# Moving the s dot products to GpSimd and ScalarE, the weight parts into the attention loop, and the denominators to tiny matmuls, in a graph-attention kernel

## The chip, the cores and the metric

The kernel runs on one core of one Trainium2 chip. The metric is the device time of one execution in microseconds (us), lower is better. TensorE is the matmul engine (PE in the rows, PEld its weight loads), VectorE is DVE, ScalarE is ACT, GpSimd is POOL, and SyncE (SP) issues the transfers. Each engine runs its own queue in order, and semaphores order them against each other.

## The reference

There are N = 1250 nodes with D = 512 features and 20,000 edges. A layer norm and a relu give h. The first layer is graph attention followed by a spline layer, the second is three graph convolutions with batch norm. The change lies in the first:

```python
HW = h @ W
s = HW @ a[:OUT_F, 0]
t = HW @ a[OUT_F:, 0]
e = leaky_relu(s[row] + t[col], negative_slope=0.2)
m = segment_max(e, row); ex = exp(e - m[row])
den = segment_sum(ex, row); att = ex / den[row]
agg = segment_sum(att[:, None] * h[col], row)
basis = _b_splines(agg, grid)
out = silu(agg) @ base_w.T + einsum('nip,oip->no', basis, spline_w)
```

## The kernel before, in words

Nodes are held as NT = 10 tiles of 128. The 20,000 edges become a dense count matrix C16 (f16), built by VectorE's one-hots and TensorE in 20 groups and copied out of PSUM by ScalarE (0 to 69 us). ScalarE's statistics, the normalised rows `hx` and their f16 high part `hH` are made beside it.

Then the attention scores. s and t are dot products of each row of hx with a row vector; TensorE made the two vectors in PSUM banks 6 and 7 and ScalarE copied them to WAB. VectorE's `projections(k, t0, t1)` makes one sum per node tile (L925). TensorE's `spread` turns a column of per-node values into a row on all partitions (L1328). VectorE takes the largest |t|, ScalarE adds twice that to the row of t (U), and per tile VectorE's `mask` (L950) and `largest` (L958) find the largest t over each node's edges. `columns` (L964 to L969) turns the maxima of a set of tiles (SETS, of 4, 3 and 3 tiles) into two columns P and Q, TensorE spreads them, ScalarE copies them out (`attention_rows`). Meanwhile TensorE transposes C16 and ScalarE copies the result to CT (`transposed`), TensorE sums the degrees with 100 matmuls of one column (`degrees`), and ScalarE sums the squares of the spline weights WKf, nine pieces of 1024 KB (`sum_squares`), from which one scale for the weights follows.

The attention loop runs n over 3 groups of destinations (G = 418 columns each) times 10 source tiles. Each iteration is `attention_sum(n+1)` (VectorE, L987), `exponentials` (ScalarE, L590), `attention_f32` (VectorE, L999: times the counts), a cast to f16 (ScalarE, L599, high part into CT) and `attention_low` (VectorE, L994, low part). In the first ten iterations VectorE also makes `hL`, the low part of the features (`feature_rest`, L1004). TensorE follows with `attend(g, k, j)`: k = 1 to 4 are the feature chunks of 128, three matmuls each, and k = 0 are the denominators, two matmuls with a matrix of ones, all of 418 columns; a group is 10 x 14 matmuls. The last three tiles of a group (LASTS) run chunk by chunk, so that chunks end one after another. VectorE then takes the reciprocal of the denominators (`denominators`, L1027 and L1029) and scales the chunks (`aggregated`, L1035).

After the loop ScalarE and VectorE split the spline weights into high and low f16 parts (`weights_high` L606, `weights_low` L1040; units 0 to 9, the others at LATE_TURN inside the turns), interleaved with `silu_of`, `silu_high` and `silu_low`. Each spline unit is 24 matmuls of 418 columns (L1482). TensorE runs four silu units first (`silu_units`), then 8 turns of two units for each group. A turn's operands go through ScalarE's `middle`, `nearest`, `clipped`, `squares_of`, `turn_high` (L620, L625, L631 and L632, L644 and L647, L665) and VectorE's `cube_outer`, `cube_inner`, `spline`, `turn_low`, `upper`, `lower` (L1048, L1051, L1055, L1072, L1083, L1089). The tiles kr, ka and kb of a turn share memory with hH and hL, so `middle(0)` waits until TensorE has finished the aggregation. Layer norm and the three graph convolutions follow.

## Time and profile before

| what | value |
|---|---|
| median of 3 runs | 684.4 us (683.07 to 684.95) |
| the profiled execution's own time | 683.7 us |
| its span, first to last instruction | 681.9 us |
| mean granted TensorE clock | 0.95 of full speed |
| busy, share of the span | TensorE 604.3 us (89%), VectorE 477.9 (70%), ScalarE 371.5 (54%), GpSimd 23.3 (3%) |
| chain that ended last, by engine | TensorE 67%, VectorE 18%, ScalarE 8%, issue 4% |

Busy time is an average over stages with different bounds. The chain is followed back from the last instruction, at each step to what released it. A matmul's end is modelled, so successive starts tell more than the duration of one. The granted clock has two levels, 2.4 GHz (1.00) and 1.2 GHz (0.50).

### The profile page before, as it was taken

Reading aid. Unit: us, or ns where it says so; the run is one execution under the profiler, and the core shown is the slowest. Engines: PE = TensorE matmul, PEld = TensorE weight load, DVE = VectorE, ACT = ScalarE, POOL = GpSimd, SP = SyncE. Lnnn points to the kernel's source line nnn. Section 1 sums busy time; section 2 is a strip of 40 time slices with the busy share of each in tenths; the row PEclk is TensorE's granted clock in tenths of the full one; section 3 lists DMA queues with packets and bytes.
Section 4 is the critical chain, followed back from the end, with each engine's and each line's share of the span. In section 5 each row is a group of like instructions: output and inputs, shape, how many; then the busy total and the mean of one; then the engine's idle time right before and its main releaser. Section 6 shows DMA issues by size and latency. Waiting matters only on the chain.

```text
span 681.9 us, 8727 instructions
## 1 busy us (share of the span) xinstructions
PE 604.3 (89%) x3437; PEld 428.2 (63%) x3437; DVE 477.9 (70%) x739; ACT 371.5 (54%) x486; POOL 23.3 (3%) x30
## 2 busy tenths in 40 slices
PE   3766655999968999999999999869999999999994
PEld 2535643555534455555555555448999899988994
DVE  7989698999785999997369865784344434542354
ACT  1798597545779998987198620328331422332111
POOL 2000000000000000000000000202300020000000
PEclk9798686999979899999999999979999999999998
DMA  8553400000040000000001000090100000001202
GB/s 278 192 186 126 195 1 0 1 1 1 0 151 0 2 1 0 1 1 1 1 1 62 1 0 1 23 369 15 62 1 1 0 1 1 1 0 56 94 38 113
DMA packets 11417, 33.73 MB, mean 49 GB/s; under 512 B 718, under 2 KB 1038, under 8 KB 11120
## 3 DMA queue, kind: packets, MB, share of 16 engines
q1 hardware_dynamic: 11376, 33.17, 13.8%
q8 instruction: 27, 0.44, 0.3%
q14 instruction: 14, 0.11, 0.1%
HBM read 24.78 MB, written 8.40 MB: 49 GB/s over the span
## 4 chain that ended last, share of the span: by engine, by line
PE 67%; DVE 18%; ACT 8%; issue 4%; DVEq 1%; ACTq 1%; DMA 0%; SPq 0%
PE bank L1482 32%; PE bank L1557 20%; PE bank L1526 12%; DVE AL L994 2%; DVE OR L847 2%; DVE OM L850 2%; DVE EX L987 1%; DVE EX L999 1%; DVE SCR L958 1%; ACT CT L599 1%; PE bank L1328 1%; ACT JSQ L532 1%; ACT WKh L606 1%; DVE RDN L1029 1%; DVE hL L1004 1%
## 5 line engine op out<-in xcount | busy, mean ns | idle before, releaser
L1482 PE MATMUL bank<-BHL,WKh 128*128 128x418 f16 x1152 | 207.1, 342 | 4.2 <-DVE BHL L1083 4.2
L1482 PEld LDWEIGHTS bank<-BHL,WKh 128*128 128x128 f16 x1152 | 112.0, 97 | 99.3 <-DVE BHL L1083 4.6
L1557 PE MATMUL bank<-CF,YL 128*128 128x418 f32 x360 | 127.5, 354 | 0.0
L1557 PE MATMUL bank<-CF,YH 128*128 128x418 f32 x360 | 126.6, 352 | 0.0
L1277 DVE TENSOR_TENSOR Z<-bank,dvb 128x418 f32<-128x418 f32 x36 | 21.3, 593 | 69.1 <-PE bank L1557 69.1
L1557 PEld LDWEIGHTS bank<-CF,YL 128*128 128x128 f32 x360 | 67.6, 188 | 1.8
L1557 PEld LDWEIGHTS bank<-CF,YH 128*128 128x128 f32 x360 | 67.7, 188 | 1.0
L784 ACT ACTIVATE bnc<-bnm,tiny 128x1 f32<-128x1 f32 x12 | 3.5, 294 | 104.9 <-DVE bnm L1283 104.9
L1335 PE MATMUL bank<-OM,OR 128*128 128x160 f16 x320 | 32.3, 268 | 19.7 <-DVE OM L850 13.7
L1228 DVE SCALAR_TENSOR_TENSOR YL<-bank,dvc,YH 128x512 fp32r<-128x512 f32 x30 | 21.9, 748 | 38.5 <-ACT YH L765 38.5
L1526 PE MATMUL bank<-GWH,XH 128*128 128x512 f32 x120 | 48.1, 401 | 0.0
L1526 PE MATMUL bank<-GWL,XH 128*128 128x512 f32 x120 | 46.9, 391 | 0.0
L1526 PE MATMUL bank<-GWH,XL 128*128 128x512 f32 x120 | 46.9, 391 | 0.0
L1335 PEld LDWEIGHTS bank<-OM,OR 128*128 128x128 f16 x320 | 27.9, 114 | 29.0 <-DVE OM L850 26.2
L1427 PE MATMUL bank<-CT,hH 128*128 128x418 f16 x120 | 41.3, 344 | 0.0
L1427 PE MATMUL bank<-CT,hL 128*128 128x418 f16 x120 | 41.2, 344 | 0.0
L1427 PE MATMUL bank<-AL,hH 128*128 128x418 f16 x120 | 41.2, 344 | 0.0
L765 ACT ACTIVATE YH<-bank,dvc 128x512 fp32r<-128x512 f32 x30 | 20.7, 692 | 33.2 <-PE bank L1526 33.2
L1089 DVE TENSOR_TENSOR BHL<-kh,BHL 128x1672 f16<-128x1672 f16 x24 | 24.7, 1029 | 19.6 <-PE bank L1482 19.6
L1482 PE MATMUL bank<-BHL,WK 128*128 128x418 f16 x144 | 28.4, 361 | 6.4 <-issue 6.4
L644 ACT ACTIVATE ks<-kx 128x836 f32<-128x836 f32 x24 | 21.5, 897 | 17.4 <-DVE kh L1072 15.9
L850 DVE TENSOR_TENSOR OM<-iota,kwin 128x2560 f16<-128x2560 f16 x20 | 29.6, 1478 | 0.0
(202 smaller groups left out, 1010.6 us busy)
## 6 DMA issues: line engine op xcount, KB each, us to landing
WKf<-in_wk SPq DMA_DIRECT2D x9, 1024.0 KB, 5.4
c_scratch<-C SPq DMA_DIRECT2D x1, 3200.0 KB, 10.9
GWf<-in_gwT SPq DMA_DIRECT2D x3, 1024.0 KB, 5.4
C<-c_scratch SPq DMA_DIRECT2D x1, 2880.0 KB, 10.4
XT<-in_xT SPq DMA_DIRECT2D x1, 2500.0 KB, 8.8
x_scratch<-XT SPq DMA_DIRECT2D x1, 2500.0 KB, 16.1
XR<-x_scratch SPq DMA_DIRECT2D x1, 2500.0 KB, 8.9
outT<-Z SPq DMA_DIRECT2D x4, 625.0 KB, 3.1
```

The costliest lines, as they stand in the source:

```text
L644: nc.scalar.activation(ks(i)[:, :], ka[:, n % 2, :], ACT.Square, scale=(1.0 / 6.0) ** 0.5)
L765: nc.scalar.mul(YH[:, t, :], bank[:, t % YB, :], dvc[:, t:t + 1]).then_inc(y_high, 1)
L847: V.tensor_tensor(fours(OR[:, buf, :, :]), rows_of(iota[:, 0:P], VIS), fanned(index, P), ALU.is_equal)
L850: V.tensor_tensor(fours(OM[:, buf, :, :]), rows_of(iota[:, :], VIS), fanned(index, MOV), ALU.is_equal).then_inc(ready, 1)
L1089: V.tensor_tensor(both(u + 1), kh[n % 2], both(u), ALU.subtract).then_inc(k_lower, 1)
L1228: V.scalar_tensor_tensor(YL[:, t, :], bank[:, t % YB, :], dvc[:, t:t + 1], YH[:, t, :].bitcast(F32), ALU.mult, ALU.subtract).then_inc(y_lo ...
L1277: V.tensor_tensor(Z[:, c, g * G:(g + 1) * G], bank[:, YB + u % YB, 0:G], dvb[:, g * G:(g + 1) * G], ALU.mult).then_inc(z_out, 1)
L1335: ins = mm(out, OR[:, buf, v0 + v, :], OM[:, buf, v0 + v, :], start=(first and v == 0), stop=(last and v == n - 1))
L1427: ins = mm(bank[:, ((DC + 1) * g + k) % 8, 0:G], lhs, m[:, j, cols], start=(j == 0 and i == 0), stop=(j == NT - 1 and i == len(parts) - 1))
L1482: ins = mm(bank[:, 4 * (g % 2) + o, 0:G], lhs, rhs, start=(u == 0 and q == 0 and i == 0), stop=(u == UNITS - 1 and q == PAIR - 1 and i == 2))
L1526: ins = mm(bank[:, t % YB, :], lhs, rhs[:, c, :], start=(c == 0 and i == 0), stop=(c == DC - 1 and i == 2))
L1557: ins = mm(bank[:, YB + u % YB, 0:G], Y[:, j, o * P:(o + 1) * P], CF[:, j, g * G:(g + 1) * G], start=(j == 0 and i == 0), stop=(j == NT - ...
```

## The change

- The ten products for s are made by GpSimd (`product`) in three buffers SH, and summed by ScalarE while it copies them in place (`projected`). GpSimd also makes hL (`feature_rest`). VectorE keeps the t sums, which read their vector from PSUM.
- The largest |t| is replaced by a bound: ScalarE takes the norm of the vector for t during the counting. The bound is added to t's column before it is spread, and the masks read the spread row from PSUM; U is gone. TensorE transposes through banks 4 and 5 alone, and spreads t, then sums degrees, behind tile 0.
- Six sums of squares move from ahead of the loop into iterations 0, 2, 4, 6, 8 and 10; the table for Exp is loaded before the first rows of P and Q.
- The denominators are made with the weights as the stationary operand and one column of ones: 80 matmuls of one column for a group (`weight_sums`), a reciprocal of 4 columns, and a spread (`sums_spread`).
- Ten high parts and eight low parts of the spline weights move into the loop; behind it stand the silu steps alone, and the order of the first turns' steps on ScalarE is changed.

```diff
+LATE_SQUARES = (0, 2, 4, 6, 8, 10)
...
+DEN_AT = 480
+BOUND = 1.02
+FIRST_HALF = 16
...
-LATE_TURN = (0, 1, 2, 3, 4, 5, 5, 6)
+LOOP_LOWS = 8
+LATE_TURN = (1, 2, 2, 3, 3, 4, 5, 6)
...
+        SH = at("SH", Z4 + 9600, [LOT, D], F32)
+        WA = at("WA", Z4 + 12552, [D], F32)
+        SCR = at("SCR", Z4 + 8320, [2, NP], F16)
...
+            def feature_rest(t):
+                pool.wait_ge(h_high, t + 1)
+                nc.gpsimd.tensor_tensor(hL[:, t, :], hx[:, t, :], hH[:, t, :], ALU.subtract).then_inc(h_low, 1)
+
+            def product(t):
+                pool.wait_ge(h_rows, t + 1)
+                if t >= LOT:
+                    pool.wait_ge(s_sums, t - LOT + 1)
+                nc.gpsimd.tensor_tensor(SH[:, t % LOT, :], hx[:, t, :], WA[:, :], ALU.mult).then_inc(s_products, 1)
+
+            pool.wait_ge(sub_counted, GROUPS)
+            pool.wait_ge(wa_set, 1)
+            for t in range(NT):
+                product(t)
+            pool.wait_ge(t_cols, 1)
+            for t in range(NT):
+                feature_rest(t)
...
-                    nc.scalar.copy(WAB[:, :, :], bank[:, 6:8, :]).then_inc(wa_set, 1)
+                    nc.scalar.copy(WA[:, :], bank[:, 6, :]).then_inc(wa_set, 1)
+                    nc.scalar.activation(JST[:, 0, :], bank[:, 7, :], ACT.Square, accum_out=tb[:, 0:1])
+                    act.drain()
+                    nc.scalar.activation(tb[:, 1:2], tb[:, 0:1], ACT.Sqrt, bias=tiny[:, 0:1], scale=BOUND * D
+                                         ).then_inc(t_bound, 1)
...
+            def projected(t):
+                act.wait_ge(s_products, t + 1)
+                nc.scalar.activation(SH[:, t % LOT, :], SH[:, t % LOT, :], ACT.Identity, accum_out=st[:, 0, t:t + 1]
+                                     ).then_inc(s_sums, 1)
+
+            for t in range(4):
+                projected(t)
+            transposed(0)
+            projected(4)
+            projected(5)
             act.wait_ge(degs_done, 1)
             nc.scalar.activation(dvc[:, :], bank[:, 3, 0:NT], ACT.Sqrt, bias=1.0).then_inc(degs_out, 1)
-            act.wait_ge(t_spread, 1)
-            act.wait_ge(t_scale, 1)
-            nc.scalar.activation(U[:, :], bank[:, 0:3, :].rearrange("p b c -> p (b c)")[:, 0:NP], ACT.Identity,
-                                 bias=tb[:, 1:2]).then_inc(t_used, 1)
-            for t in range(5, NT):
+            for t in range(1, NT):
                 transposed(t)
+                if t <= 4:
+                    projected(t + 5)
 
...
+            nc.scalar.activation(mv[:, 0, 0:1], tiny[:, 0:1], ACT.Exp)
+            attention_rows(0)
...
             attention_rows(1)
-            sum_squares(7, JSQ2)
-            sum_squares(8, JSQ2)
-            nc.scalar.activation(mv[:, 0, 0:1], tiny[:, 0:1], ACT.Exp)
-            attention_rows(2)
...
+            def weights_high(u):
+                act.wait_ge(wscale_set, 1)
+                act.wait_ge(agg_unit, DC + 1)
+                if u >= 2:
+                    act.wait_ge(wk_low, u - 1)
+                nc.scalar.mul(weights(u)[:, 0, :], raw_weights(u), wsc[:, 0:1]).then_inc(wk_high, 1)
...
+                if n == 0:
+                    attention_rows(2)
+                if n in LATE_SQUARES:
+                    sum_squares(3 + LATE_SQUARES.index(n), JSQ3)
+                if FIRST_HALF <= n < FIRST_HALF + LATE:
+                    weights_high(n - FIRST_HALF)
...
             silu_of(0, 0)
-            weights_high(0)
-            weights_high(1)
+            silu_of(0, 1)
             silu_high(0, 0)
-            weights_high(2)
-            silu_of(0, 1)
-            weights_high(3)
...
             act.wait_ge(agg_unit, (DC + 1) * NG)
-            act.wait_ge(agg_out, DC)
             middle(0)
+            nearest(0)
+            clipped(0)
             middle(1)
-            nearest(0)
             nearest(1)
-            clipped(0)
-            weights_high(8)
-            weights_high(9)
...
-                    V.tensor_tensor_reduce(out=JH[:, t, :], in0=hx[:, t, :], in1=WAB[:, k, :], scale=1.0, scalar=0.0,
+                    V.tensor_tensor_reduce(out=JH[:, t, :], in0=hx[:, t, :], in1=bank[:, 6 + k, :], scale=1.0, scalar=0.0,
...
+            dve.wait_ge(t_bound, 1)
+            V.tensor_scalar(mx[:, 3, :], st[:, 1, :], tb[:, 1:2], None, ALU.add).then_inc(t_cols, 1)
...
-            projections(0, 0, 6)
-
+            dve.wait_ge(sub_counted, GROUPS)
             dve.wait_ge(t_spread, 1)
             trow = bank[:, 0:3, :].rearrange("p b c -> p (b c)")[:, 0:NP]
-            V.tensor_reduce(tb[:, 0:1], trow, AX, ALU.max, apply_absolute_value=True)
-            dve.drain()
-            V.tensor_scalar(tb[:, 1:2], tb[:, 0:1], 2.0, 1e-30, ALU.mult, ALU.add).then_inc(t_scale, 1)
...
-                V.tensor_scalar(MSK[:, s % 2, :], C16[:, s, :], 1.0, None, ALU.min).then_inc(mask_set, 1)
+                if s >= MASKS:
+                    dve.wait_ge(masked, s - MASKS + 1)
+                V.tensor_scalar(MSK[:, s % MASKS, :], C16[:, s, :], 1.0, None, ALU.min).then_inc(mask_set, 1)
...
-                V.tensor_tensor_reduce(out=SCR[:, :], in0=MSK[:, s % 2, :], in1=U[:, :], scale=1.0, scalar=0.0,
+                V.tensor_tensor_reduce(out=SCR[:, s % 2, :], in0=MSK[:, s % MASKS, :], in1=trow, scale=1.0, scalar=0.0,
...
             mask(0)
             for i in range(NG):
                 for t in range(*SETS[i]):
                     largest(t)
+                if i == 0:
+                    dve.wait_ge(s_sums, NT)
+                    V.tensor_scalar(mx[:, 1, :], st[:, 0, :], tb[:, 1:2], None, ALU.subtract)
+                    dve.drain()
                 columns(i)
+                if i == 0:
+                    dve.wait_ge(degs_out, 1)
+                    V.reciprocal(dvc[:, :], dvc[:, :]).then_inc(dvc_set, 1)
...
-            def feature_rest(t):
-                dve.wait_ge(h_high, t + 1)
-                V.tensor_tensor(hL[:, t, :], hx[:, t, :], hH[:, t, :], ALU.subtract).then_inc(h_low, 1)
...
+                dve.wait_ge(agg_unit, (DC + 1) * g + 3)
+                V.tensor_scalar(RDC[:, g, :], bank[:, att_bank(g, 0), DEN_AT:DEN_AT + len(PARTS)], 1e-30, None, ALU.max
+                                ).then_inc(den_out, 1)
+                dve.wait_ge(den_out, g + 1)
+                V.reciprocal(RDC[:, g, :], RDC[:, g, :]).then_inc(den_cols, 1)
+
+            def denominator_row(g):
                 if g >= 1:
                     dve.wait_ge(agg_out, DC * g)
-                V.tensor_scalar(RDN[:, :], bank[:, u % 8, 0:G], 1e-30, None, ALU.max).then_inc(den_out, 1)
-                dve.wait_ge(den_out, g + 1)
-                V.reciprocal(RDN[:, :], RDN[:, :]).then_inc(rden_set, 1)
+                dve.wait_ge(den_spread, g + 1)
+                V.tensor_copy(RDN[:, :], bank[:, att_bank(g, 0), 0:G]).then_inc(rden_set, 1)
...
             for n in range(NG * NT):
                 if n + 1 < NG * NT:
                     attention_sum(n + 1)
-                if n < NT:
-                    feature_rest(n)
-                if n == 3:
-                    dve.wait_ge(squares, KB)
-                    V.tensor_reduce(wsc[:, 0:1], wss[:, :], AX, ALU.add).then_inc(sumsq_set, 1)
                 if n >= 1:
                     attention_low(n - 1)
                 attention_f32(n)
-                if n == 9:
+                if n == 11:
+                    dve.wait_ge(squares, KB)
+                    V.tensor_reduce(wsc[:, 0:1], wss[:, :], AX, ALU.add).then_inc(sumsq_set, 1)
+                if n == 13:
                     weight_scale()
-                if n == 12:
+                if n == 14:
                     denominators(0)
+                if n == 15:
+                    denominator_row(0)
                     aggregated(0, 0)
-                if n == 13:
                     aggregated(0, 1)
+                if n == 16:
                     aggregated(0, 2)
-                if n == 14:
                     aggregated(0, 3)
+                if FIRST_HALF < n <= FIRST_HALF + LOOP_LOWS:
+                    weights_low(n - FIRST_HALF - 1)
+                if n == 22:
+                    denominators(1)
                 if n == 23:
-                    denominators(1)
+                    denominator_row(1)
                     aggregated(1, 0)
...
-            weights_low(0)
-            weights_low(1)
             silu_low(0, 0)
-            weights_low(2)
-            weights_low(3)
             silu_low(0, 1)
-            weights_low(4)
-            weights_low(5)
             denominators(2)
+            denominator_row(2)
+            for u in range(LOOP_LOWS, LATE):
+                weights_low(u)
             silu_low(1, 0)
+            silu_low(1, 1)
             for c in range(DC):
                 aggregated(2, c)
-            weights_low(6)
-            weights_low(7)
-            silu_low(1, 1)
-            weights_low(8)
-            weights_low(9)
...
             for t in range(NT):
                 for b in range(2):
-                    if t >= 2:
-                        pe.wait_ge(tposed_out, 2 * t + b - 3)
+                    if t >= 1:
+                        pe.wait_ge(tposed_out, 2 * t + b - 1)
                     for s in range(5):
-                        ins = nc.tensor.transpose(bank16[:, 4 + 2 * (t % 2) + b, s * P:(s + 1) * P],
+                        ins = nc.tensor.transpose(bank16[:, 4 + b, s * P:(s + 1) * P],
                                                   C16[:, 5 * b + s, t * P:(t + 1) * P], ident16[:, :])
                     ins.then_inc(tposed, 1)
-                if t == 1:
-                    degrees(0, NT).then_inc(degs_done, 1)
-                if t == 2:
+                if t == 0:
                     pe.wait_ge(t_cols, 1)
-                    spread(0, st[:, 1, :], 0, NT).then_inc(t_spread, 1)
-
-            pe.wait_ge(dvc_set, 1)
-            pe.wait_ge(t_used, 1)
-            spread(0, dvc, 0, NT).then_inc(dv_spread, 1)
-            pe.wait_ge(tposed_out, 2 * NT)
+                    spread(0, mx[:, 3, :], 0, NT).then_inc(t_spread, 1)
+                    degrees()
...
+                hi, lo = CT[:, j, cols], low_weights(g)[:, j, :]
+                fh, fl = (h[:, j, (k - 1) * P:k * P] for h in (hH, hL))
+                parts = [(fh, hi), (fh, lo), (fl, hi)]
                 for i, (lhs, m) in enumerate(parts):
-                    ins = mm(bank[:, ((DC + 1) * g + k) % 8, 0:G], lhs, m[:, j, cols],
+                    ins = mm(bank[:, att_bank(g, k), 0:G], lhs, m,
...
+            def weight_sums(g):
+                for i, c0 in enumerate(PARTS):
+                    out = bank[:, att_bank(g, 0), DEN_AT + i:DEN_AT + i + 1]
+                    for j in range(NT):
+                        for low in range(2):
+                            m = low_weights(g)[:, j, c0:c0 + P] if low else CT[:, j, g * G + c0:g * G + c0 + P]
+                            ins = mm(out, m, ones16[:, 0:1], start=(j == 0 and low == 0), stop=(j == NT - 1 and low == 1))
+                ins.then_inc(agg_unit, 1)
+
+            def sums_spread(g):
+                pe.wait_ge(den_cols, g + 1)
+                for i, c0 in enumerate(PARTS):
+                    ins = mm(bank[:, att_bank(g, 0), c0:c0 + P], down(RDC[:, g, i:i + 1]), ident[:, :], start=True, stop=True)
+                ins.then_inc(den_spread, 1)
...
+                    for k in range(1, DC + 1):
+                        if j == 0:
+                            if g == 1 and k == DC:
+                                pe.wait_ge(rden_set, 1)
+                            if g == 2:
+                                pe.wait_ge(agg_out, k)
+                                pe.wait_ge(rden_set, 2)
                         attend(g, k, j)
-                    if g == 0 and j == 4:
-                        pe.wait_ge(sumsq_set, 1)
-                        mm(bank[:, 5, 0:1], ones[:, :], wsc[:, 0:1], start=True, stop=True).then_inc(sumsq_done, 1)
                 if g == 0:
-                    pe.wait_ge(wscale_set, 1)
                     pe.wait_ge(h_low, NT)
-                for k in range(DC + 1):
+                for k in range(1, DC + 1):
                     for j in range(NT - LASTS, NT):
                         pe.wait_ge(att_low, g * NT + j + 1)
                         attend(g, k, j)
+                    if g == 0 and k == 1:
+                        pe.wait_ge(sumsq_set, 1)
+                        pe.wait_ge(pq_set, NG)
+                        mm(bank[:, 2, 0:1], ones[:, :], wsc[:, 0:1], start=True, stop=True).then_inc(sumsq_done, 1)
+                    if k == 2:
+                        if g >= 1:
+                            pe.wait_ge(agg_out, DC * g)
+                        weight_sums(g)
+                    if k == 3:
+                        sums_spread(g)
 
...
-            pe.wait_ge(den_out, NG)
-            pe.wait_ge(agg_out, 2 * DC + 1)
+            pe.wait_ge(rden_set, NG)
+            pe.wait_ge(agg_out, 2 * DC)
...
```

## Rows read from the trace of the kernel before

**Rows 1.** Windows: stretch, length, busy (instructions) of PE, PEld, DVE, ACT, POOL; clock; DMA

```profile
143.20:192.90 49.70, 49.64 (x281) 27.29 (x279) 43.71 (x69) 31.19 (x46) 0.00 (x0) 1.00 0.00 1
192.90:199.20 6.30, 0.00 (x0) 0.02 (x1) 6.03 (x6) 2.53 (x4) 0.11 (x1) 0.88 0.82 288
199.20:219.00 19.80, 19.74 (x96) 10.01 (x96) 13.03 (x14) 19.77 (x23) 0.00 (x0) 0.87 0.09 38
219.00:223.10 4.10, 0.00 (x0) 0.00 (x0) 2.96 (x4) 4.10 (x6) 0.00 (x0) 0.81 0.00 0
223.10:231.60 8.50, 8.49 (x34) 4.08 (x35) 8.50 (x10) 8.50 (x11) 0.00 (x0) 0.69 0.00 0
224.00:442.00 218.00, 217.06 (x1206) 117.73 (x1204) 175.43 (x204) 144.08 (x165) 4.83 (x3) 0.99 0.02 6
```

**Rows 2.** Timeline of VectorE, 72 to 114 us

```profile
72.89 0.08 DVE L925 DVE_READ_ACCUMULATOR2_ANT st<- 128x1 f32 x1
...
87.75 0.83 DVE L950 TENSOR_SCALAR MSK<-C 128x1280 f16<-128x1280 f16 x2
...
90.43 1.49 DVE L958 CUSTOM_DVE_ANT_0 SCR<-MSK,U 128x1280 f32<-128x1280 f16 x1
...
92.37 1.48 DVE L958 CUSTOM_DVE_ANT_0 SCR<-MSK,U 128x1280 f32<-128x1280 f16 x1
...
108.86 0.15 DVE L969 SCALAR_TENSOR_TENSOR mx<-st,mx 128x3 f32<-128x3 f32 x1
...
113.70 0.60 DVE L999 SCALAR_TENSOR_TENSOR EX<-EX,CT 128x418 f32<-128x418 f32 x1 [2.91 <-ACT EX L590]
```

**Rows 3.** Chain of waits, 108 to 224 us: start, us, what

```profile
108.86 2.00 ACT JSQ L532 x2
...
110.88 1.28 ACT L585
...
212.15 0.89 ACT kx L620
...
219.33 0.79 ACT kh L665
...
222.11 0.95 DVE BHL L1083
```

**Rows 4.** Timeline of VectorE in the attention loop

```profile
148.33 0.59 DVE L1035 TENSOR_TENSOR AGG<-bank,RDN 128x418 f32<-128x418 f32 x1
...
155.03 0.59 DVE L999 SCALAR_TENSOR_TENSOR EX<-EX,CT 128x418 f32<-128x418 f32 x1
...
156.73 0.59 DVE L999 SCALAR_TENSOR_TENSOR EX<-EX,CT 128x418 f32<-128x418 f32 x1
```

**Rows 5.** Timeline of TensorE, 72 to 83 us

```profile
73.06 1.97 PE L1389 MATMUL bank<-ones,C 128*128 128x1 f16 x67
78.02 1.01 PE L1389 MATMUL bank<-ones,C 128*128 128x1 f16 x33 [2.99 <-issue]
...
79.92 3.27 PE L1328 MATMUL bank<-ident,st 128*128 128x128 f32 x20
```

**Rows 6.** GpSimd's elementwise work and VectorE's row beside it

```profile
3.81 1.27 DVE L828 TENSOR_SCALAR BF<-thr,dF 80x81 f16<-80x81 f32 x2
3.82 1.03 POOL L462 COPY AB<-acol 128x1024 f32<-128x1024 f32 x1
...
429.67 4.52 POOL L469 TENSOR_TENSOR GWL<-GWf,GWH 128x2048 fp32r<-128x2048 f32 x1 [236.65 <-ACT GWH L742]
...
465.33 1.62 POOL L484 TENSOR_TENSOR CF<-CF,ident 128x128 fp32r<-128x128 f32 x2 [23.90 <-ACT CF L760]
467.64 0.46 POOL L484 TENSOR_TENSOR CF<-CF,ident 128x128 fp32r<-128x128 f32 x1 [0.70 <-ACT CF L760]
```

**Rows 7.** Timeline of ScalarE, statistics and copies

```profile
18.02 0.63 ACT L508 ACTIVATE JST<-hx 128x512 f16<-128x512 f32 x1
...
87.12 6.11 ACT L555 COPY CT<-bank 128x640 f16<-128x640 f16 x10
```

135 lines of the change are left out of this document (56 added, 79 removed).

## The prediction

> **What bounds the kernel now.** I read the page, then the chain of waits, then windows of each engine, then the timelines from 66 to 224 us. From 223.1 us the chain is almost all TensorE; in 224 to 442 us it is busy for 217.06 of 218 us [rows 1]. Nothing behind 442 us is edited, so what the change is worth is how much earlier the first spline unit starts than 223.10 us, plus TensorE time saved behind it.
>
> Ahead of that point three parts follow one another. (a) 66.5 to 113.7: VectorE bounds. Ten sums for t end at 72.97, the masks begin at 87.75, the last column work ends at 109.01, and the loop's first weight product comes at 113.70, after VectorE idled 2.91 us [rows 2]: ScalarE still had two sums of squares, 2.00 us in a row of the chain, and a table load of 1.28 [rows 3]. (b) 116.2 to 192.85, aggregation: TensorE bounds, 281 matmuls in 49.64 of 49.70 us, 0.177 each [rows 1]. ScalarE and VectorE finish their loop around 180, unused slack. (c) 192.9 to 223.1: TensorE idles 6.3 us, runs the 96 silu matmuls in 19.8, and idles 4.1 again. It restarts at the lower clock of 1.2 GHz: 34 matmuls in 8.5 us where 48 fit at 0.177 [rows 1].
>
> **The change, part (a).** Three things leave VectorE ahead of the masks: the ten s products, the maximum of |t|, and the wait for ScalarE's U. The bound now comes from ScalarE during counting, where its extra square, drain and root fall into an idle stretch before group 13; I cost them at nothing (about 0.6 us if that cover went).
>
> t sums end at 72.97 as before; reading the weight row from PSUM is costed at nothing, since in the loop AGG<-bank costs 0.59, as L999 does with SBUF operands [rows 4]. TensorE spreads t right behind tile 0's transposes: 73.4 + 3.1 (20 records, 3.27 with overlap [rows 5]) = 76.5. The masks can start there instead of at 87.75. Ten tiles cost 1.93 us each (mask 0.4 plus product, the pitch of the two SCR rows in [rows 2]), and the column work that ends each set about 0.6 (four small ops behind a product, the last of them at 108.86).
>
> The first `columns` now waits for all ten s sums. GpSimd: a two-input op costs 0.46 at 128 columns and 4.52 at 2048 [rows 6], so about 1.27 at 512; ten from 69.4 (last counts copied) end near 83 to 85. ScalarE: free at 71.8, each sum is 0.63 [rows 7]. It does six and tile 0's copies by 77.7, waits for degrees (100 tiny matmuls at 0.029 [rows 5], behind the spread: 79.2), then four rounds of two copies (0.60 each, ten took 6.11 [rows 7]) and one sum: 1.85 each, the first with 0.6 for the transposes, so S = 87.0. VectorE would have finished four tiles at 84.5. So 2.5 us of VectorE idle is the new wait, and ScalarE is late with it. The 2.99 us stall inside the degrees [rows 5] waited for nothing that the profile shows and ended at 78.02; in the new order most degrees come after that time, so I leave it out; kept, S would be up to 3 later. From S: 0.3 + columns 0.64 + reciprocal 0.13 + 5.8 + 0.62 + 5.4 + 0.62 = 13.5, last column work ends at X = 100.5.
>
> **GpSimd beside the masks.** That sum ignores the one thing the trace warns of. At 3.81 two VectorE TENSOR_SCALARs of 81 columns took 1.27 us, where a mask of 1280 columns takes 0.4, and GpSimd's 1.03 us copy ran from 3.82 to 4.85: they look held until that copy was done. In the other direction two 0.46 us GpSimd adds took 1.62 us beside VectorE's XL, which has two SBUF inputs [rows 6]. The mask is a TENSOR_SCALAR, and GpSimd now has 20 ops of 1.27 us queued, 10 products and 10 `feature_rest`. If a mask waits for the GpSimd op in progress, then after each mask GpSimd does two (2.54) before the next: cycle 2.95 instead of 1.93. Replayed: mask 0 +0.7, masks 2 to 4 +1.0 each, set 0 ends at 88.4, past S; the small TENSOR_SCALAR behind S +1.1; masks 5 to 7 together +2.2; GpSimd is through at 98.4. X = 88.4 + 13.5 + 1.1 + 2.2 = 105.2. The bounds are 0 (100.5) and VectorE held until GpSimd is empty (masks from about 96: X = 116). I take 105.2, by the row at 3.81.
>
> The Trainium skill (GPSIMD Engine Reference, section Key points) says GpSimd shares its SBUF interfaces with VectorE and contends with VectorE ops that use both ports or have two SBUF inputs. The rows at 3.81 and 465.33 agree. By that rule masks are hit and the PSUM-fed products are not, which is the 105.2; without it the sum is 4.7 lower.
>
> **Loop head and group 0.** The exponential table is loaded earlier. From X: spread of set 2 done at X+1.7, first weight product X+1.4, then the copy, two PQ copies (0.75) and the first moved square: that square ends at X+5.1. With six squares (every other iteration) a pair of iterations costs the ring low, weight product, cast once, 1.70 with its latencies (an iteration's pitch, [rows 4]), then the square 2.0, then ScalarE's exp and cast of the iteration that waited, 1.07: 4.77. Five pairs: the last square ends at X+29.0. That is slower per iteration than before (2.39 against 2.17), and moving `hL` to GpSimd buys nothing here. TensorE now stands in its queue in front of the norm matmul until all squares are in, having done only 9 of its last 36 matmuls; in the 9 us before it works 1.6 us, so it starts again at 1.2 GHz. Behind it: VectorE reaches `denominators(0)` 7.15 us after the last square (three iterations and `weight_scale`, 1.35), the denominator spread 1.1, nine matmuls 1.6, so group 0 ends 10.0 after it, plus 2.0 for the slow clock (bounds 0 and 4; the restart at 223.1 lost 14 × 0.177 = 2.5 [rows 1]).
>
> **Groups 1 and 2.** Removed: 20 matmuls, 3.5 us each group. Added: 80 tiny matmuls, 2.35 at 0.029 (that row is at 1.2 GHz, so 1.2 is the other bound; I take 2.1), and 8 records of the spread, 0.163 each at 1.2 GHz [rows 5], 1.3; I take 1.1. 120 × 0.177 = 21.2. Each group 24.4 against 24.8. VectorE carries eight low and ScalarE ten high parts in slack: iterations 17 to 24 cost 2.8 us, end at about X+78, while TensorE ends at X + 29.0 + 12.0 + 48.8 = X+89.8 = 195.0. So aggregation ends 2.1 later than now.
>
> **Part (c), where the gain is.** TensorE needs only `rden_set` 3 and AGG of group 1, both there: the 6.3 us idle goes. The weight parts no longer stand in ScalarE's queue. From TensorE's end: middle, nearest, two of clipped 3.5; middle, nearest 1.8; squares 1.6; clipped 1.8; middle, nearest 1.8; squares 1.6, clipped 1.8, middle 0.9, high 0.8 (0.89 and 0.79 per op, [rows 3]) = 15.6; then VectorE low, inner cube, upper 2.9: 18.5. Silu matmuls need 96 × 0.177 = 17.0, so a 1.5 us wait is left. First unit at 195.0 + 18.5 = 213.5 instead of 223.1: −9.6. It starts at full clock: −2.5. A turn then costs VectorE 7.4 to 8.6 (one or two low parts) against TensorE's 48 × 0.177 = 8.5, so TensorE stays the bound.
>
> **Sum.** −12.1 on the profiled execution (span 681.9, time 683.7): 671.6. The median of the runs is 0.7 above it: 672.3, I say 672.
>
> **Rivals.** (1) GpSimd does not hold masks: X = 100.5, all 4.7 earlier, 667.5. For it: the row at 3.81 is a single case with another output type. (2) TensorE's clock falls at the denominator sums too, or in the wait before the first turn: 2.5 each time, up to four times, typically three, 679.5. Against it: 1.6 us of idle is short beside the 4.1 after which the clock was at 0.81 [rows 1]. (3) Slower than before: Square is not in the table that Exp uses, so each of the six squares in the loop loads twice, 12 × 1.28 = 15.4 us on the path that ends at the last square: 687.5. It decides from 12.1 us on, so from ten loads. Square runs without a load behind the first, the Sqrt and the Silu load in this trace, which speaks against it. The Trainium skill (ScalarE: Activation LUTs, section Table sets) lists relu, copy, identity and abs as in every set, and does not name square; no run here shows it under Exp. (4) GpSimd starves the masks or its ops cost double: X = 111 to 116, 678 to 683, the change does hardly what it says. The Trainium skill (GPSIMD Engine Reference, section Engine selection) puts two-input elementwise work on VectorE, GpSimd being about twice as slow; the 1.27 at 512 columns against VectorE's 0.59 at 418 agrees.
>
> **Chances.** Sum 0.47, rival 1 0.27, rival 2 0.12, rival 3 0.05, rival 4 0.09. A measurement can tell 0.3%, 2 us, from no change. Faster: all but rival 3 and a third of rival 4: 0.92; same 0.03; slower 0.05. Range: rival 1 with denominator sums and cold clock at their lower bounds (−2.7 and about −1) gives 664; rival 2 gives 680.
>
> **What would show it.** Right: `MSK` ops with 1 us of wait in front while `SH` or `hL` runs on GpSimd; VectorE at the s sums about when ScalarE is, at 87 to 89; masks from 76.5; a loop pair of 4.8 us with a 2 us square; TensorE nearly idle for 9 us ahead of the norm matmul; silu matmuls following group 2 without a gap; first spline unit at 213, at full clock; everything behind 442 moved as a block. Wrong: table loads in the loop; S past 90; a spline stage in which VectorE or ScalarE is waited for; a clock below 1 in groups 1 and 2.

## The result and the profile after

The changed kernel takes 673.68 us (median of 4 runs, 670.24 to 674.46) against 684.12 us before (4 runs, 683.07 to 684.95): a ratio of 0.984, 95% interval 0.980 to 0.988. The prediction said 672 (664 to 680). The profiled execution took 674.32 us with a span of 672.5.

Windows of TensorE after the change (stretch, length, busy and instructions, granted clock, DMA); they answer to [rows 1]:

```profile
108.00:120.00 12.00, 9.68 (x52) 0.91 0.00 0
120.00:134.00 14.00, 10.01 (x53) 1.00 0.01 2
134.00:147.00 13.00, 11.02 (x110) 0.50 0.01 1
147.00:196.00 49.00, 49.00 (x421) 0.99 0.00 1
196.00:205.00 9.00, 9.00 (x52) 1.00 0.76 281
205.00:216.00 11.00, 9.02 (x51) 1.00 0.01 4
216.00:224.50 8.50, 8.35 (x48) 1.00 0.00 1
```

TensorE now loses time at 120 to 134 us (4 us idle) and at half clock until 147.5. The 6.3 us idle and the 20 us at 0.87 that [rows 1] show behind aggregation are gone, and the first spline unit starts at 216.15 instead of 223.10, with 48 matmuls in 8.5 us instead of 34.

VectorE's timeline (start, length, what), ahead of the loop; it answers to [rows 2]:

```profile
73.62 0.66 DVE L973 TENSOR_SCALAR mx<-st,tb 128x10 f32<-128x10 f32 x1
...
74.43 1.08 DVE L976 TENSOR_TENSOR mx<-st,mx 128x10 f32<-128x10 f32 x1
79.07 1.97 DVE L984 TENSOR_SCALAR MSK<-C 128x1280 f16<-128x1280 f16 x2 [3.56 <-PE bank L1365]
...
82.37 0.48 DVE L984 TENSOR_SCALAR MSK<-C 128x1280 f16<-128x1280 f16 x1
...
84.18 1.30 DVE L984 TENSOR_SCALAR MSK<-C 128x1280 f16<-128x1280 f16 x1
85.40 1.48 DVE L992 CUSTOM_DVE_ANT_0 SCR<-MSK,bank 128x1280 f16<-128x1280 f16 x1
...
89.28 0.82 DVE L1013 TENSOR_SCALAR mx<-st,tb 128x10 f32<-128x10 f32 x1
90.18 1.03 DVE L998 TENSOR_TENSOR mx<-mx 128x4 f32<-128x4 f32 x1
91.30 1.04 DVE L1000 SCALAR_TENSOR_TENSOR mx<-mx 128x4 f32<-128x4 f32 x1
92.41 1.03 DVE L1002 TENSOR_TENSOR mx<-st,mx 128x4 f32<-128x4 f32 x1
...
98.69 0.48 DVE L984 TENSOR_SCALAR MSK<-C 128x1280 f16<-128x1280 f16 x1
...
100.61 0.16 DVE L998 TENSOR_TENSOR mx<-mx 128x3 f32<-128x3 f32 x1
...
106.93 0.15 DVE L1003 SCALAR_TENSOR_TENSOR mx<-st,mx 128x3 f32<-128x3 f32 x1
```

GpSimd's timeline in the same stretch:

```profile
70.52 11.65 POOL L500 TENSOR_TENSOR SH<-hx,WA 128x512 f32<-128x512 f32 x9 [65.65 <-ACT C L548]
83.87 1.26 POOL L500 TENSOR_TENSOR SH<-hx,WA 128x512 f32<-128x512 f32 x1 [1.70 <-ACT SH L610]
85.09 11.92 POOL L494 TENSOR_TENSOR hL<-hx,hH 128x512 f16<-128x512 f32 x10
```

Read the two together. GpSimd works until 97.0, with a pause from 82.2 to 83.9. While it works a mask takes up to 1.32 us, and most small operations with two SBUF inputs take 1.03. Afterwards the same operations take 0.48 and 0.16, and so does the one mask that starts in the pause (82.37). The hold shows as a longer operation, not as idle time in front of it. The product SCR, whose second input is in PSUM, takes 1.47 or 1.48 throughout. The last column work ends at X = 107.1 (109.0 before).

The chain of waits, from X to the end of aggregation (start, us, what):

```profile
107.14 2.94 PE bank L1365 x12
...
133.74 2.01 ACT JSQ L578 x2
136.57 3.16 PE bank L1463 x9
139.73 2.11 PE bank L1474 x80
141.84 3.16 PE bank L1463 x9
145.00 1.71 PE bank L1480 x8
146.70 20.15 PE bank L1463 x111
166.85 1.98 PE bank L1474 x80
168.83 1.61 PE bank L1463 x9
...
171.33 19.62 PE bank L1463 x111
```

Six squares pace the loop, a pair of iterations every 4.57 us. Behind the last one nine matmuls take 3.16 us, where nine at full clock take 1.61: that is what the low clock of 1.2 GHz costs them.

### The profile page after: what moved, and what is told of

It reads as the page before. It is cut to its first block, busy times and chain, and to the rows that moved or that the text cites. A ratio compares the mean times of both kernels' runs of the same rounds, so it can differ in the third digit from the quotient of the medians.

```text
span 672.5 us, 9166 instructions
## 1 busy us (share of the span) xinstructions
PE 604.3 (90%) x3641; PEld 432.0 (64%) x3641; DVE 465.1 (69%) x711; ACT 375.8 (56%) x508; POOL 48.1 (7%) x50
## 4 chain that ended last, share of the span: by engine, by line
PE 76%; DVE 12%; ACT 7%; issue 3%; DVEq 1%; ACTq 1%; DMA 0%; SPq 0%
PE bank L1538 32%; PE bank L1613 20%; PE bank L1582 12%; PE bank L1463 8%; DVE OR L889 2%; DVE OM L892 2%; ACT JSQ L578 2%; DVE MSK L984 1%; PE bank L1365 1%; DVE JH L967 1%; PE bank L1474 1%; DVE SCR L992 1%; ACTq L555 1%; ACT JST L559 1%; DVE XL L1259 1%
## 5 line engine op out<-in xcount | busy, mean ns | idle before, releaser
L1538 PE MATMUL bank<-BHL,WKh 128*128 128x418 f16 x1152 | 204.6, 339 | 2.1 <-DVE BHL L1124 2.1
L515 POOL TENSOR_TENSOR GWL<-GWf,GWH 128x2048 fp32r<-128x2048 f32 x3 | 13.8, 4586 | 294.1 <-ACT GWH L784 222.9
```

The source lines that it names most:

```text
L515: nc.gpsimd.tensor_tensor(GWL[:, :, :], GWf[:, :, :], GWH[:, :, :].bitcast(F32), ALU.subtract).then_inc(gw_low, 1)
L1538: ins = mm(bank[:, 4 * (g % 2) + o, 0:G], lhs, rhs, start=(u == 0 and q == 0 and i == 0), stop=(u == UNITS - 1 and q == PAIR - 1 and i == 2))
```

## Experiments

Each kernel was timed in 3 or 5 rounds beside the kernel before, and is compared by its ratio to that, since the median of before moved from 684.1 to 684.9 between the chip sessions. The interval of the changed kernel overlaps those of hL behind the masks, norm matmul later and three squares ahead, so the 1 to 4 us between these medians are not clear of the noise by themselves. X is the end of the last column work and T the start of the first turn unit, both in the profiled execution.

| kernel | median us | ratio, 95% interval | X | T |
|---|---|---|---|---|
| changed kernel | 673.68 | 0.984 (0.980 to 0.988) | 107.1 | 216.2 |
| hL behind the masks | 672.89 | 0.983 (0.981 to 0.985) | 102.9 | 215.3 |
| s on VectorE | 667.50 | 0.975 (0.973 to 0.977) | 103.8 | 212.8 |
| s and hL on VectorE | 665.58 | 0.972 (0.971 to 0.974) | 100.6 | 206.4 |
| before, hL alone on GpSimd | 690.95 | 1.008 (1.006 to 1.011) | 119.8 | 231.2 |
| norm matmul later | 670.71 | 0.980 (0.978 to 0.982) | 106.5 | 212.3 |
| three squares ahead | 669.93 | 0.979 (0.977 to 0.981) | 106.1 | 210.4 |
| weight parts behind the loop | 681.12 | 0.997 (0.995 to 0.999) | 106.1 | 219.2 |

T can be some 3 us off what a median says: s on VectorE was profiled in an execution of 670.56 us, the longest of its five, and s and hL on VectorE in one of 664.10, the shortest of its four.

### What GpSimd's operations cost

**hL behind the masks.** GpSimd still makes the ten s products, but waits with hL until all masks are through.

```diff
-            pool.wait_ge(t_cols, 1)
+            pool.wait_ge(masked, NT)
```

> The changed kernel with GpSimd's ten hL subtractions behind the last mask instead of beside the masks; all else as changed. Theory (a VectorE mask, a small TENSOR_SCALAR and a small two-input op wait for the GpSimd op in progress): the masks behind 87 us lose their 0.7 to 0.8 us each, the column ops of set 0 fall from 1.03 to 0.16 us, and the last column work ends near 102 instead of 107.1; the contention moves into the attention loop, which has 1.2 us of VectorE idle in each pair of iterations and so hides some of it. Time about 669 to 671. Rival (the ops are long for another reason, for instance PSUM or ScalarE's copies): still 1.0 to 1.3 us with GpSimd idle, last column work at 107, time 673 to 674.

The masks behind set 0 fell back to 0.48 us and X came 4.1 us earlier, at 102.9. The time hardly moved (0.983 against 0.984, and 672.9 us where 669 to 671 were expected), because hL now ran from 100.6 to 114.2 beside the head of the loop. VectorE's timeline there:

```profile
101.83 1.04 DVE L1002 TENSOR_TENSOR mx<-st,mx 128x3 f32<-128x3 f32 x1
...
102.86 3.01 DVE L1029 SCALAR_TENSOR_TENSOR EX<-PQ,mx 128x418 f32<-128x418 f32 x2
105.80 1.54 DVE L1041 SCALAR_TENSOR_TENSOR EX<-EX,CT 128x418 f32<-128x418 f32 x1
...
108.72 1.54 DVE L1036 TENSOR_TENSOR AL<-EX,CT 128x418 f16<-128x418 f32 x1
```

An operation of 0.59 us takes 1.54. The last square ended at 135.9, against 135.7 in the changed kernel: all 4.1 us were given back. So the two stretches pay about the same price for ten GpSimd operations, some 4 us.

**s on VectorE.** The products and sums for s stand behind the t sums on VectorE, out of PSUM like those; GpSimd makes hL alone.

```diff
-            for t in range(NT):
-                product(t)
...
-            for t in range(4):
-                projected(t)
...
             dve.wait_ge(sub_counted, GROUPS)
+            projections(0, 0, NT)
+            V.tensor_scalar(mx[:, 1, :], st[:, 0, :], tb[:, 1:2], None, ALU.subtract)
             dve.wait_ge(t_spread, 1)
```

> The changed kernel with the ten s products and sums on VectorE again, behind the t sums, and none on GpSimd and ScalarE; hL stays on GpSimd. Theory (the move of s buys nothing, since VectorE waits 3.56 us for the spread of t anyway and GpSimd's ops hold the masks): products fill 74.5 to 80.7, masks start 1.6 us later than in the changed kernel, but GpSimd is through at about 86 and the column ops cost 0.16 us; last column work near 104.5 (107.1 as changed), time about 671. Rival (taking 6.1 us off VectorE is worth its 6.1): last column work at 111 or later, time 677 or more.

Ten more sums on VectorE, at 0.61 us each, made the kernel 0.009 x 684 = 6 us faster. In the profiled executions X comes 3.3 us earlier and T 3.4. The rest of the 6 us is not located: the profiled execution took 670.56 us at a mean granted clock of 0.947, the other four 666.8 to 667.6 us at 0.952 to 0.956, and of those there is no trace. VectorE starts the masks only 1.6 us later (80.7 against 79.1): 3.56 us of the sums' 6.1 fall into its wait for the spread of t, and the last small operation ahead of them (L976, here L967) takes 0.17 instead of 1.08. In return the small column operations of set 0 cost 0.16 instead of 1.03, and hL, from 74.0 to 85.7, runs half beside the sums, which it doesn't hold (0.68 us, started every 0.61, as without GpSimd), and half beside two groups of masks, which it does:

```profile
79.57 0.68 DVE L958 CUSTOM_DVE_ANT_0 JHS<-hx,bank 128x512 f16<-128x512 f32 x1
...
80.34 0.45 DVE L970 TENSOR_SCALAR mx<-st,tb 128x10 f32<-128x10 f32 x1
80.70 2.88 DVE L977 TENSOR_SCALAR MSK<-C 128x1280 f16<-128x1280 f16 x2
83.51 1.47 DVE L985 CUSTOM_DVE_ANT_0 SCR<-MSK,bank 128x1280 f16<-128x1280 f16 x1
...
84.91 1.15 DVE L977 TENSOR_SCALAR MSK<-C 128x1280 f16<-128x1280 f16 x1
```

**s and hL on VectorE.** As the last, and hL is made by VectorE in the first ten iterations. GpSimd has no part.

```diff
+                if n < NT:
+                    dve.wait_ge(h_high, n + 1)
+                    V.tensor_tensor(hL[:, n, :], hx[:, n, :], hH[:, n, :], ALU.subtract).then_inc(h_low, 1)
```

> The changed kernel with the s products and sums on VectorE (behind the t sums) and hL on VectorE too, one tile in each of the first ten iterations of the loop. GpSimd has no part between 70 us and the aggregation. Theory (a mask waits for the GpSimd operation in progress): with s on VectorE and hL still on GpSimd the last column work came at 103.8, with the masks held 3.4 us in all (2.88 for two, 1.15 for one, against 0.48 each); without hL every mask takes 0.4 to 0.5 and the last column work comes at 100.4. In the loop hL (0.5 each) hides behind the 2 us squares, a pair of iterations stays near 4.6, the last square comes 28.7 behind the last column work, at 129.1, and the time is 3.4 below the 667.5 of the kernel with s alone moved back: 664. Rival 1 (the masks were slow for another reason, such as data not there yet): last column work still at 103.8, time 667.5. Rival 2 (hL costs the loop what it takes): each pair 5.6 instead of 4.6, last square 33.7 behind the column work, time 669.

X fell by 3.3 us to 100.6, and the last square ended at 129.0, 28.4 behind X: hL in the loop is hidden behind the squares. The median is 665.58, the lowest of all kernels, 1.9 us below s on VectorE. Masks in VectorE's timeline, none held:

```profile
80.08 0.89 DVE L974 TENSOR_SCALAR MSK<-C 128x1280 f16<-128x1280 f16 x2
80.88 1.48 DVE L982 CUSTOM_DVE_ANT_0 SCR<-MSK,bank 128x1280 f16<-128x1280 f16 x1
...
82.29 0.49 DVE L974 TENSOR_SCALAR MSK<-C 128x1280 f16<-128x1280 f16 x1
```

T fell by more than X, 6.4 us. Of the other 3.1, 2.9 are TensorE's clock behind the last square. Its windows in this kernel (columns as in the windows of the changed kernel):

```profile
132.00:134.00 2.00, 2.00 (x51) 0.75 0.00 0
134.00:147.00 13.00, 13.00 (x110) 1.00 0.01 2
```

The clock is back at full by 134, and group 0 ends at 138.9, 9.9 behind the last square. In the changed kernel and with s on VectorE the clock stays at half for some 12 us behind the last square, and group 0 ends 12.9 and 12.8 behind it.

**hL alone on GpSimd, in the kernel before.**

```diff
+            pool.wait_ge(dvc_set, 1)
+            for t in range(NT):
+                pool.wait_ge(h_high, t + 1)
+                nc.gpsimd.tensor_tensor(hL[:, t, :], hx[:, t, :], hH[:, t, :], ALU.subtract).then_inc(h_low, 1)
...
-                if n < NT:
-                    feature_rest(n)
```

> The kernel before with one edit: hL leaves VectorE's loop and is made by GpSimd as soon as the degree roots are there, which is beside the masks of sets 1 and 2. Theory (masks wait for the GpSimd operation in progress, and aggregation is bound by TensorE from 120 us on): about six masks cost 0.8 us more each, last column work at 113 to 115 instead of 109.0, the loop is shorter by up to 5 us on VectorE but TensorE does not care, time 687 to 689. Rival 1 (GpSimd holds nothing): last column work at 109.0, time 684, or up to 3 lower where the head of the loop is VectorE's. Rival 2 (a loop without hL feeds TensorE sooner and pays for the masks): 682 to 684.

It is 6 us slower than before, more than expected, and X comes 10.8 later where 4 to 6 were expected. GpSimd runs from 89.7 to 107.0, beside the masks of set 0, and here the product is held too. Its operand U lies in SBUF:

```profile
93.76 1.32 DVE L954 TENSOR_SCALAR MSK<-C 128x1280 f16<-128x1280 f16 x1
95.00 2.44 DVE L962 CUSTOM_DVE_ANT_0 SCR<-MSK,U 128x1280 f32<-128x1280 f16 x1
...
107.25 0.49 DVE L954 TENSOR_SCALAR MSK<-C 128x1280 f16<-128x1280 f16 x1
107.65 1.49 DVE L962 CUSTOM_DVE_ANT_0 SCR<-MSK,U 128x1280 f32<-128x1280 f16 x1
```

2.44 while GpSimd works, 1.49 afterwards; and GpSimd's own operations take 1.73 each (17.27 for ten) instead of 1.19. With the spread row read from PSUM the same product stayed at 1.47. That part of the change protects VectorE from GpSimd. The product's output also differs (f32 here, f16 in the changed kernel), and no run separates the two.

### The order of the loop

**Weight parts behind the loop.** The ten high and ten low parts go back between the silu steps and behind them, as before the change.

```diff
-                if FIRST_HALF <= n < FIRST_HALF + LATE:
-                    weights_high(n - FIRST_HALF)
...
-                if FIRST_HALF < n <= FIRST_HALF + LOOP_LOWS:
-                    weights_low(n - FIRST_HALF - 1)
...
+            weights_low(0)
+            weights_low(1)
             silu_low(0, 0)
```

> The changed kernel with the ten high and ten low weight parts behind the loop again, interleaved with the silu steps as before. Theory (their place is what shortens the way from the end of aggregation to the first unit): aggregation ends at the same time or up to 1 us earlier, the first spline unit comes 27 to 30 us behind it instead of 19.1, TensorE idles before the silu units or before the first turn, time 682 to 685, all of the gain gone. Rival (the cheaper denominators and the silu order give the gain): first unit within 3 us of the changed kernel's, time 674 to 677.

This one takes back 0.013 x 684 = 9 us by the ratios, 7.4 by the medians, of the 10.4 gained. Windows of this kernel (PE, PEld, DVE, ACT, POOL, clock):

```profile
180.00:196.00 16.00, 12.62 (x138) 8.42 (x136) 10.17 (x11) 15.97 (x19) 0.00 (x0) 0.92 0.00 1
196.00:206.00 10.00, 10.00 (x56) 5.38 (x55) 7.94 (x10) 8.54 (x10) 0.11 (x1) 0.97 0.69 252
206.00:219.00 13.00, 8.97 (x51) 4.69 (x49) 8.72 (x10) 12.97 (x16) 0.00 (x0) 0.93 0.01 5
219.00:226.00 7.00, 6.82 (x26) 3.17 (x27) 7.00 (x9) 7.00 (x8) 0.00 (x0) 0.64 0.00 1
```

TensorE idles 3.4 and 4.0 us, with ScalarE full: first for VectorE's last column reciprocal, which stands behind low weight parts, then for the first turn. Aggregation ends at 197.8 and the first turn unit comes 21.4 behind it, less than the 27 to 30 expected; 3.4 us of the loss stand ahead of that end. It comes at 219.2 instead of 216.15 although X is 1.0 earlier and the clock was back at full by 139, and it runs at the low clock: 26 matmuls in 7 us. The 2 to 3 us of gain that are left are not taken apart: the cheaper denominators and the new order on ScalarE have no run of their own.

**Norm matmul later.** It stands behind the denominator sums of group 0, and `denominators(0)` two iterations earlier.

```diff
-                    if g == 0 and k == 1:
-                        pe.wait_ge(sumsq_set, 1)
...
                         weight_sums(g)
+                        if g == 0:
+                            pe.wait_ge(sumsq_set, 1)
...
+                if n == 12:
+                    denominators(0)
                 if n == 13:
                     weight_scale()
```

> The changed kernel with the norm matmul behind the denominator sums of group 0 instead of behind chunk 1, and VectorE's column reciprocal at iteration 12 and the row at 14 (14 and 15 as changed). Theory (TensorE stands in front of the norm matmul, goes cold and does 27 matmuls and the sums after it): chunk 2 and the sums run at 133 to 137, the granted clock stays high, group 0 ends near 143 instead of 148.3, everything behind it 4 to 5 us earlier, time about 669. Rival (group 0 ends with the loop iterations of VectorE whatever TensorE does): group 0 ends within 1 us of 148, time 673 to 674.

3.0 us faster than the changed kernel by the medians, 2.7 by the ratios. TensorE no longer waits for the last square, has the low clock in parts of 132 to 142 us instead of from 134 to 147.5, and ends group 0 at 143.8 instead of 148.7.

**Three squares ahead.** ScalarE idles at 101.4 to 103.0 and 103.9 to 107.7 in the changed kernel.

```diff
-LATE_SQUARES = (0, 2, 4, 6, 8, 10)
+LATE_SQUARES = (0, 2, 4)
...
+            act.wait_ge(c16_out, 16)
+            sum_squares(3, JSQ3)
             attention_rows(1)
+            sum_squares(4, JSQ3)
+            sum_squares(5, JSQ3)
...
-                if n == 11:
+                if n == 6:
                     dve.wait_ge(squares, KB)
```

> The changed kernel with three of the six squares of the loop made ahead of it, in ScalarE's idle stretches at 101.4 to 103.0 and 103.9 to 107.7; the squares left are in iterations 0, 2 and 4, and VectorE adds the nine sums up in iteration 6 instead of 11. Theory (six squares on ScalarE pace the loop and hold TensorE back): the last square comes 3 x 4.57 earlier after the last column work (28.65 - 13.7 = 15), three pairs of iterations take 3.4 instead of 4.57, so that VectorE reaches the denominators of group 0 3.5 us earlier, TensorE has no 2 us gaps left and stays at full clock in the 9 us behind the norm matmul (up to 2 us more): 668 to 670.2. Rival 1 (TensorE's own work bounds group 0): same as the changed kernel, 673.7. Rival 2 (a square ahead of the loop delays the first exponentials by as much as it saves): 673 to 675.

As expected, 3.7 us faster by the medians, 3.4 by the ratios: TensorE is busy for 12.83 of 120 to 134 us and keeps the full clock there. It now waits later, 2.88 us until 138.9 for VectorE's reciprocal of iteration 14, and the clock falls, to 0.59 from 138 to 140.

### Putting the parts together

Both moves, of the norm matmul and of squares, were then added to the kernels without s on GpSimd, alone or together.

```diff
-FIRST_HALF = 16
+FIRST_HALF = 20
```

(This edit, in the last two alone, delays the weight parts in the loop by four iterations.)

> The changed kernel with s back on VectorE (that alone gave 667.5 against 673.7) and the norm matmul behind the denominator sums of group 0 with the denominators two iterations earlier (that alone gave 670.7). Theory: the two lie one behind the other on the same path (last column work, then the end of group 0), so the gains add: 667.5 - 3.0 = 664.5, first turn unit at 212.8 - 3.8 = 209.0. Rival: both gains come from the same wait of TensorE (its idle time and the low clock behind it), and the second brings nothing: 667.

> All the parts that helped together: s and hL on VectorE (665.6 alone), the norm matmul behind the denominator sums with the denominators two iterations earlier, and three of the six squares ahead of the loop (669.9 alone, where TensorE waited 2.9 us for VectorE's reciprocal in iteration 14, which the earlier denominators take away). Theory: last column work at 100.5 as with all on VectorE; last square 15 behind it; behind the squares an iteration with hL costs VectorE 2.2 and one without 1.7, so iteration 12 comes some 28 behind the column work and group 0 ends 3 to 5 us earlier than with all on VectorE: 661 to 663. Rival 1 (with the squares gone the loop is VectorE's, and hL's ten steps of 0.5 now stand on the path): only 0 to 2 gained, 664 to 665.6. Rival 2 (TensorE's own matmuls bound group 0, so nothing is left to gain): 665.6.

> The same with hL left on GpSimd beside the masks, as the changed kernel has it: s on VectorE, norm matmul and denominators moved, three squares ahead. The masks pay 3.4 us (last column work at 103.8) and the loop is 0.5 an iteration shorter where no square covers it, seven of ten iterations. Theory: the two cancel to within 1 us of the kernel with hL on VectorE, 662 to 664. Rival (hL is covered in the loop all the same, as with six squares): 2 to 3 slower than that kernel, 664 to 666.

> The kernel with hL on GpSimd, s on VectorE, the norm matmul and denominators moved and three squares ahead (666.2), with one more edit: the weight parts in the loop begin at iteration 20 instead of 16. There TensorE lost 2.2 us in group 1 to VectorE's reciprocal and spread row, with VectorE busy throughout and five low parts of 1.27 us in front of them. Theory (VectorE's queue had become the bound in the middle of the loop): the gaps of TensorE at 155 to 165 us go, 664. Rival (the low parts then pile up at the end of the loop and make VectorE late for the silu steps or the last denominators): 666 or more.

> s and hL on VectorE (665.6 alone), the norm matmul and denominators moved, one square ahead of the loop in the stretch where ScalarE has nothing to do (101.4 to 103.0 in the changed kernel, 98.8 to 100.7 with all on VectorE), and the weight parts from iteration 20. Three squares ahead had held the first exponentials back until 105.5 while the last column work was done at 100.2; one square ends before it. Theory: first exponentials at about 101.5 as with all on VectorE alone, the last square 4.57 earlier (about 124.3), denominator sums of group 0 at 129 to 130 instead of 132.7, no wait of TensorE behind them: 662 to 663. Rival (TensorE's idle time ahead of the sums only moves, or VectorE is late for group 1 all the same): 665 to 666.

| kernel | median us | ratio, 95% interval | X | T |
|---|---|---|---|---|
| s on VectorE, norm later | 667.21 | 0.974 (0.973 to 0.976) | 103.4 | 209.4 |
| s and hL on VectorE, norm later, three squares ahead | 668.26 | 0.975 (0.973 to 0.978) | 100.2 | 208.9 |
| s on VectorE, norm later, three squares ahead | 666.15 | 0.974 (0.973 to 0.976) | 103.0 | 206.4 |
| the same, weight parts from iteration 20 | 668.15 | 0.976 (0.973 to 0.978) | 104.2 | 210.5 |
| s and hL on VectorE, norm later, one square ahead, parts from 20 | 667.17 | 0.974 (0.972 to 0.976) | 101.1 | 209.9 |

The gains that were added up here failed to add: the medians lie 2.2 to 5.3 us above the top of what each theory expected. None of the five beats s and hL on VectorE alone (0.972), and their intervals overlap its own. Two of the profiles show where a gain went. With three squares ahead, s on VectorE, the sums of group 0 start at 129.9 instead of the 132.7 of s and hL on VectorE alone, but the reciprocal of group 1 comes no earlier. TensorE's rows of that kernel:

```profile
159.64 1.16 PE L1474 MATMUL bank<-ident,RDC 128*128 128x128 f32 x8 [1.63 <-DVE RDC L1058]
...
162.99 0.34 PE L1457 MATMUL bank<-CT,hH 128*128 128x418 f16 x1 [0.60 <-DVE RDN L1064]
```

and of that with the weight parts from iteration 20 (VectorE's, then TensorE's timeline):

```profile
160.19 0.16 DVE L1055 TENSOR_SCALAR RDC<-bank 128x4 f32<-128x4 f32 x1 [3.02 <-PE bank L1468]
```

```profile
180.35 0.35 PE L1457 MATMUL bank<-CT,hH 128*128 128x418 f16 x1 [0.73 <-DVE AL L1029]
...
182.06 0.35 PE L1457 MATMUL bank<-CT,hH 128*128 128x418 f16 x1 [1.00 <-DVE AL L1029]
```

VectorE is busy for 36.84 of 38.00 us from 122 to 160 in the first of these, and makes that reciprocal at 159.2; with s and hL on VectorE alone at 159.1, and TensorE arrives with it: 40.00 of 40 us busy from 150 to 190. Delaying the weight parts brought VectorE to iteration 22 early, where it stood for 3.02 us with its parts still to do, and TensorE then waited for the last weight products at 180. Up to the reciprocal of group 1 the two engines are level in these kernels, so a cut on TensorE's side alone goes into a wait for VectorE. Behind it VectorE has slack (31.99 of the 40 us busy with s and hL on VectorE alone). That does not explain all five: with s on VectorE and the norm matmul later, T came at 209.4, as expected (209.0), and 3.4 before T of s on VectorE alone; but that kernel was profiled in its slowest execution, and the medians are the same.

## Why the prediction was right

**Sums for t and the spread.** The t sums ended at 73.5 (72.97 predicted), the PSUM operand cost nothing. TensorE's spread took 4.65 us instead of 3.1, at the low clock throughout. The prediction had read the spread of [rows 5] as one at 1.2 GHz; in that trace the clock is 0.50 from 80 to 81 us and 1.00 from 82 to 83. The column of t ahead of it was held too (0.66 us instead of some 0.2). So the masks began at 79.07 instead of 76.5.

**The new wait at the s sums.** ScalarE finished them at 89.1, two us past the predicted 87.0: it idled 2.83 us ahead of the degrees. VectorE, held by GpSimd, came at 89.28 (88.4 predicted) and didn't wait. The predicted stall was covered by the predicted delay.

**GpSimd beside the masks.** This was the step with the largest doubt. The mechanism was right. The masks lost 4.1 us over what they take later in the same trace (5.9 predicted in the replay), the small TENSOR_SCALAR 0.6 (1.1), and the three two-input column operations of set 0, which the replay did not hold, 0.87 each, 2.6. So 7.3 in all stand against 7.0: that the sum was right is luck, its parts were not. An unheld tile costs 1.81 instead of 1.93, 1.2 for the ten. Set 0 ended 0.9 later than predicted, and X followed 17.8 behind it instead of 16.8: X = 107.1 instead of 105.2, the first miss, +1.9: 2.6 from the late start of the masks and 0.3 from GpSimd, less the 1.2. The Trainium skill (GPSIMD Engine Reference, section Key points) names VectorE operations in a 2-port mode or with two SBUF inputs as those that contend. For two inputs these runs agree on both sides: SCR at 2.44 us with its operand in SBUF and at 1.47 with it in PSUM. The masks have one SBUF input and are held; in which mode they run no trace shows.

**Loop head and group 0.** Last square at X + 28.65 (29.0). The group ended at 148.7, 12.9 behind it (12.0), with the clock at half from 134 to 147.5. The path was another than predicted. The sum goes through VectorE's iterations to `denominators(0)`, 7.15 behind the square, and VectorE was there on time (142.45); but TensorE reached the spread only at 145.0, since its two chunks of nine matmuls took 3.16 us each at the low clock. The predicted 10.0 without the slow clock fits the kernel with s and hL on VectorE (9.9, full clock by 134). So the slow clock's term, 2.0 within bounds of 0 and 4, was 3.0 at least, since that kernel had some 4 us of it too.

**Groups 1 and 2.** A group took 24.3 and 24.1 us (24.4); aggregation ended at 197.0, X + 89.95 (X + 89.8). Group 0's 0.9 too much was made up by 0.35 at the squares and 0.4 here.

**Part (c).** The first turn unit followed 19.1 behind (18.5), after an idle time of 2.1 (1.5), at full clock: +0.6, the second miss. Behind it the kernel is 2.45 us shorter (2.5). That most of the gain lies here is borne out by the kernel with the weight parts put back, which gives back 7.4 of 10.4 us by the medians. The misses add to 2.7 over the predicted 671.6, with rounding the 674.3 of the profiled execution.

**Rivals.** Rival 1, GpSimd holds nothing: refuted by the masks here and, beyond the profile, by the runs in which they shrink as it stops. Its X of 100.5 was reached with GpSimd idle and all its work on VectorE. Rival 2, the clock falls at the denominator sums too: no, at full clock from 148. Rival 3, table loads at the squares: the chain has two JSQ rows of 2.00 us in all for each square and no load between them. Rival 4, GpSimd's operations cost double: 1.29 us each for the products and 1.19 for hL, where 1.27 was predicted.

What the prediction did not ask is whether GpSimd's share was worth having. It called moving hL worth nothing; by the medians it costs 1.9 us (3.3 at X), and s on GpSimd another 6, of which 3.4 show in the profiled executions. The change gained in spite of them.

**What stays open.** The distance between X and the first turn unit is 109.1 in the changed kernel, 109.0 with s on VectorE and 105.8 with s and hL there. The difference is how long the clock stays low behind the last square; what ends the low stretch after some 4 us in one kernel and some 12 in the others no run here shows. So in the 1.9 us between the medians of the last two the masks' hold and the clock are not separated. Whether the kernel with s and hL on VectorE is really 1 to 3 us ahead of the five combinations is within their intervals.

## What to carry to other kernels

Before giving GpSimd elementwise work, look at what VectorE does in that stretch: PSUM-fed products go on undisturbed, while masks, most small two-input operations and weight products each wait for the GpSimd operation in progress, and moving the work to another stretch here only moved the loss. Put it where VectorE reads PSUM, or leave it on VectorE in iterations that wait for another engine anyway. When two engines are level over a stage, single gains on one of them are not to be added up: look first at when the other one reaches its next hand-over.

## What the hardware showed that was not expected

- A VectorE operation of 128x4 with two SBUF inputs takes 0.16 us alone and 1.03 beside GpSimd. What is lost is up to one GpSimd operation (1.2 to 1.3 us) whatever the size of VectorE's: 0.87 here, 0.67 to 0.84 for a mask, 0.95 for a weight product. One of the four small operations of set 0, right behind three held ones, took 0.15 all the same.
- GpSimd loses too, most where VectorE's operation is long and reads SBUF twice: ten hL took 11.9 us beside masks and PSUM-fed products, 13.6 beside the weight products, 17.3 beside masks and products with both inputs in SBUF.
- 80 matmuls of one column take 1.98 us at full and 2.11 at half clock: their pace hardly depends on the clock, where nine of 418 columns take 1.61 and 3.16.
